# A graph network on one core: GpSimd's gathers wait for the whole group in front from the first column on, and for a count of used columns

## What is computed

```python
x = x + gat(h)        # two graph attention layers (3 heads x 32, then 1 x 32), softmax over the edges of a dst
x = x + rgcn(h)       # two relation passes, 8 relations: mean per (dst, relation), times W[r], summed
x = x + dynamics(h)   # msg = w * h[src] * h[dst] / (5 + 0.9 h[src] + 0.1 h[dst]), summed at src
x = x + relation(h)   # msg = (h[src] @ W_rel[type]) * e, summed at dst, 90 relation types
```

## Time and profile before

| What | us |
|---|---|
| median of 3 runs (lowest, highest) | 6640.55 (6635.97, 6644.13) |
| span of the profiled execution, first to last instruction | 6645.3 |
| GpSimd busy | 4320.0 (65%) |
| VectorE busy | 3659.5 (55%) |
| TensorE busy (matmuls) | 2965.9 (45%) |
| ScalarE busy | 1167.0 (18%) |
| mean of a gather: GAT 1, GAT 2, relation pass 1, pass 2, layer 4 | 1.097, 1.062, 1.058, 1.002, 1.001 |

### The profile page before, as it was taken

How to read it: one execution, slowest core, us unless ns; L and a number is a source line. 1 busy time by engine, 2 the same in 40 slices (tenths; PEclk the granted TensorE clock), 3 DMA queues, 4 the chain that set the end, 5 groups by cost and what they waited for, 6 DMA issues and landing times. The chain is left out here.

```text
span 6645.3 us, 44822 instructions
## 1 busy us (share of the span) xinstructions
PE 2965.9 (45%) x13056; PEld 2260.1 (34%) x13056; DVE 3659.5 (55%) x8917; ACT 1167.0 (18%) x1912; POOL 4320.0 (65%) x3949
## 2 busy tenths in 40 slices
PE   5798699974444344447655443111111002544000
PEld 2477555543333233346644333111111001433000
DVE  8855499976555566654347667433322068876000
ACT  0265454532222233211111100000000000000000
POOL 4666555557762776376657665888888823766776
PEclk9899899985666555556667665555555555776555
DMA  2122222221110322123222212222222234211001
GB/s 41 22 62 70 56 67 67 66 66 12 20 17 14 89 60 65 47 64 100 84 87 60 64 53 72 52 36 36 44 27 27 5 96 154 57 50 37 7 7 44
DMA packets 283354, 350.11 MB, mean 53 GB/s; under 512 B 133518, under 2 KB 204432, under 8 KB 281970
## 3 DMA queue, kind: packets, MB, share of 16 engines
q1 hardware_dynamic: 112158, 295.24, 13.2%
q0 software_dynamic: 169376, 41.40, 7.8%
q10 hardware_dynamic: 1576, 10.60, 0.7%
HBM read 231.06 MB, written 122.29 MB: 53 GB/s over the span
## 5 line engine op out<-in xcount | busy, mean ns | idle before, releaser
L2352 POOL DMA_INDIRECT acc<-l_rows,l_uniq x392 | 624.1, 1592 | 121.0 <-issue 108.6
L2573 POOL DMA_INDIRECT l_ring<-t_last,idx x392 | 392.4, 1001 | 366.5 <-ACTq L2568 207.6
L521 POOL DMA_INDIRECT pay<-in_x,gidx x392 | 460.1, 1174 | 235.4 <-DMA pay<-in_x,gidx 114.3
L2393 PE MATMUL ps_l<-l_msg,l_alike 128*128 128x16 f32 x784 | 176.3, 376 | 962.4 <-DVE l_msg L2456 962.4
L1487 POOL DMA_INDIRECT g_ring<-t_gat,idx x392 | 416.1, 1062 | 278.7 <-issue 110.1
L1817 POOL DMA_INDIRECT r_ring<-t_rel,idx x392 | 414.6, 1058 | 254.6 <-issue 110.3
L809 POOL DMA_INDIRECT t_sort<-pay,c_pos x392 | 384.8, 982 | 296.3 <-DVE c_pos L875 196.3
L901 PE MATMUL ps_c<-plane,c_hit 128*128 128x400 f32 x1568 | 542.6, 499 | 1.2 <-ACT c_hit L827 1.2
L2128 POOL DMA_INDIRECT r_ring<-t_rel,idx x392 | 392.7, 1002 | 224.4 <-issue 110.4
L2338 POOL DMA_INDIRECT l_ring<-t_mix,idx x392 | 426.3, 1087 | 154.6 <-issue 119.1
L2393 PEld LDWEIGHTS ps_l<-l_msg,l_alike 128*128 128x128 f32 x784 | 171.0, 331 | 967.7 <-DVE l_msg L2456 967.7
(11 more groups left out here) (529 smaller groups left out, 8145.0 us busy)
## 6 DMA issues: line engine op xcount, KB each, us to landing
c_rows_d<-row_dst SPq DMA_DIRECT2D x98, 256.0 KB, 3.3
l_keys<-row_at SPq DMA_DIRECT2D x49, 512.0 KB, 4.2
l_typs<-row_typ SPq DMA_DIRECT2D x49, 512.0 KB, 3.7
g_hs<-t_gat SPq DMA_DIRECT2D x30, 660.0 KB, 4.7
acc<-r_zero SPq DMA_DIRECT2D x60, 320.0 KB
t_rel<-r_row SPq DMA_DIRECT2D x30, 640.0 KB, 3.5
r_hs<-t_rel SPq DMA_DIRECT2D x30, 640.0 KB, 4.7
d_gain<-acc SPq DMA_DIRECT2D x30, 640.0 KB, 6.0
```

The lines of the kernel that those rows point to most:

```text
L521: pool.indirect_dma_start(pay[:, s, 8:PAY], None, x, bass.IndirectOffsetOnAxis(gidx[:, s:s + 1], 0)).then_inc(gat_in[s // BATCH], 16)
L2352: pool.indirect_dma_start(acc[r], bass.IndirectOffsetOnAxis(uniq[:, s:s + 1], 0), rows[:, (s // ES) % RR, s % ES, :], None, compute_op=ALU.add
L2573: pool.indirect_dma_start(ring[:, s, :], None, t_last, bass.IndirectOffsetOnAxis(idx2[:, s:s + 1], 0)).then_inc(gat_in[s // BATCH], 16)
```

## The change

`RUN` becomes 0: the wait is for the group directly in front at every eighth column, from the first possible one on. A new helper `credit` adds, at each eighth column past a lead, a wait for a count of used columns: at most `lead` columns are asked for beyond those used. It stands ahead of `paced` in GAT 1 (96 columns, by blocks of 48 mixed), GAT 2 (64, by blocks of 40), relation pass 1 (64, by 8), relation pass 2 (32, by 4) and layer 4 (40, by 8). The ring holds go. The node stage and layer 3 get the new `RUN` alone.

```diff
-RUN = 160
+RUN = 0
...
+def credit(engine, used, s, lead, per):
+
+    if s % BATCH == 0 and s > lead:
+        engine.wait_ge(used, -(-(s - lead) // per))
...
                     for s in range(EARLY, T):
+                        credit(pool, mix_ok, s, 2 * EW, EW)
                         paced(pool, gat_in, s, EARLY)
...
                     for s in range(T):
-                        if s % QN == 0 and s >= NR * QN:
-                            hold(pool, ring_free, s // QN - NR + 1)
+                        credit(pool, ring_free, s, 64, QN)
                         paced(pool, gat_in, s)
...
                         for s in range(T):
-                            if s % QN == 0 and s >= NR * QN:
-                                i = s // QN - NR
-                                hold(pool, expand_ok, first[i] + subs[i])
+                            credit(pool, expand_ok, s, 64, ES)
                             paced(pool, gat_in, s)
...
                     for s in range(T):
-                        if s % QN == 0 and s >= NR * QN:
-                            i = s // QN - NR
-                            hold(pool, lift_ok, first[i] + subs[i])
+                        credit(pool, taken, s, 32, ES)
                         paced(pool, gat_in, s)
...
                     for s in range(T):
+                        credit(pool, mats_used, s, 40, ES)
                         paced(pool, gat_in, s)
```

## The result

The changed kernel takes 6881.51 us (median of 4 runs, 6878.73 to 6890.48), the kernel before in the same comparison 6642.34 (4 runs). The ratio is 1.0366, interval 1.0351 to 1.0381: 239 us more. The forecast was 6909 us, range 6820 to 6945: 28 us high. The profiled execution took 6881.99 us with a span of 6880.0.

The account below looks back on a forecast made before the run. GpSimd's gathers were taken to bound all five streams, so each delay ends its stage later. Landing waits of 188 us plus credits of 81 make 269, added to the median 6640.55: 6909 us, range 6820 to 6945.

Parts of the forecast that it names:

- What bounds each stage: GpSimd's gathers set the end of all five streams; in the node stage VectorE's end covers 4 us, 4 come through.
- GAT 1, layer 3 and layer 4, landing waits: New waits for the group in front cost 17 us in GAT 1, 14 in layer 3, 34 in layer 4.
- GAT 2, landing waits: First groups, behind a 5.6 MB load, cost 12.6 us and the 16 groups after 22.4: together 35.
- stalls rival: Gathers of the five streams meet VectorE less and give back at most 234 us, so 6594 us; chance 0.02.
- Relation passes, landing waits: 19 new waits in each pass at 2.05 and 2.39 us cost 39 and 45 us; 26 each by the lowest price.
- Credits: A second wait costs about 0.45 us at each place in the five streams although long met: 81 us.
- can pass meanwhile: Relation pass 2's credits: 12 of 18 us taken, as the 0.45 us can pass while a load delays a landing.
- That credits never hold GpSimd: In the five streams every used count is reached before its gather, by 24.8 us at the tightest, in relation pass 2.
- Lockstep: Rival: each chunk's store and load meet a landing, relation passes pay 3.5 us a wait, 48 more, 6957 us; chance 0.06.
- absorbed: Rival: the engines behind the gathers have slack, so late gathers cost nothing and it stays at 6640 us; chance 0.02.

Follow-up runs that it names:

- e7: The changed kernel with the landing wait put ahead of the credit wait in the five streams, on a quick chip: 6794.74 us, 1.0232 of the kernel before.
- e6: The changed kernel, unchanged, run again on a quick chip: 6881.38 us, 1.0359 of the kernel before.
- e5: The kernel before, unchanged, run again on a quick chip for its trace: 6640.61 us.
- e12: The changed kernel, credits included, with its landing wait moved to columns with remainder 4, on a slow chip: 7411.22 us, 0.9525 of the kernel before.
- e3: The changed kernel with the landing wait ahead of the credit wait, on a slow chip: 6771.81 us, 0.869 of the kernel before.
- e8: The kernel before with the landing wait for the group in front moved to columns with remainder 4, on a quick chip: 6454.35 us, ratio 0.9721.

## Why the prediction was right, and where its steps were not

Total, sign and the split were right: 154 us for the landing waits against 188, 87 for the credits against 81. It rested on a stage-by-stage reading of who waits last, and that stood: no stage absorbed anything. That the credits came out within 6 us is partly luck, as layer 4 at 18 us too much and relation pass 2 at 20 us too little cancel. Step by step:

- **What bounds each stage.** Right for the five streams. Wrong in the node stage, where I let VectorE's 1543.1 set the end and so took 4 us. It lost 9.0, all of GpSimd's delay. Behind the last gather the raw events show a wait for its landing (to 1538.87) and then a drain of 4.63 us (1539.06 to 1543.69, in the changed kernel 1548.58 to 1553.20) before the block may end. GpSimd set the end in both; VectorE's idle time before its next operation grew from 1.93 to 10.99 us. I had read only the busy instructions.
- **GAT 1, layer 3 and layer 4, landing waits.** 17, 14 and 34 forecast, 19.3, 13.7 (over layer 3's first 80 gathers) and 35.9 measured.
- **GAT 2, landing waits.** The gaps at the eighth columns grew from 8.9 + 54.7 to 48.9 + 49.7 us, exactly the 35 of the sum, with the first groups as worked out. But the gathers' mean fell from 1.063 to 1.030 us, and 392 of those are 12.9 us: the stalls rival, which I had given 0.02 and argued away with two halves of one stream, was true in part: in e7 it gave back 12 us over the five streams, nearly all in GAT 2. Of the 37 us in the changed kernel of the first comparison it is the smaller share; from e7 to e6 the gathers' busy time falls by another 23 us, 19 of them in layer 4, where the credits move the gather past VectorE's operation.
- **Relation passes, landing waits.** Mis-sized: 39 and 45 against 19.2 and 27.2. The price taken was the mean over the paced half (2.05 and 2.39 us), which holds the late landings: in the trace of e5, relation pass 1 has seven gaps over 3 us in its 29 waits. I took it that the new waits would meet as many. In e7 there are four in 48: gaps below column 160 grew by 30.8 us and those above it shrank by 13.2. Late landings belong to the traffic that they meet, and did not multiply with the waits. The lowest price, 26 us each, was nearer.
- **Credits.** The price was right (0.46 us in the medians of layer 4's gaps, 1.65 to 2.11; 0.48 from landing to gather at every place) and so was its reason in outline. By stage it was not even: layer 4, where the delay let the gather miss VectorE's operation, cost 1.4 instead of 19; relation pass 2 cost 32.0 instead of 12. There the mean gap from column 160 on rose from 2.52 to 3.25 us, more than the wait. What I deducted as "can pass meanwhile" does not pass: the 0.74 us begin at the landing, however late it is. The rest are landings that came later still (from the last gather's start to its group's landing 3.55 us in e7, 3.81 in e6, means of the 22 groups that can be read); why they do was not tried. GAT 2 cost 27.9 instead of 16, of which 6.2 are slower gathers (1.030 to 1.046 us).
- **That credits never hold GpSimd.** Right on the quick chips: the gather follows its landing by the same 0.74 us (at most 1.05) at every place with a credit. On a slow chip it is wrong (e12, 56.2 us).
- **Lockstep, absorbed.** Neither happened on the whole; relation pass 2's credits are what there is of the first.

The range was fit for the chips of the first comparison. It says nothing of the slow chips. The changed kernel did not run there; e3's 6772 and 87 us more for the order would be an estimate of 6860, some 12% below the kernel before on such a chip. By that estimate the change gives back on such a chip several times what it costs on a quick one, if the loss is there without the recording.

No version was best everywhere: e8 with 6454 us is the fastest measured on a quick chip, e3 with 6772 on a slow one. On the slow ones e8 was not run; with credits the same wait gave 7411.

## What to carry to other kernels

Pace a stream by a group that has had time to land: the same wait four gathers later cost nothing, where right behind its group it cost 1.3 us or more each time. If two waits precede an instruction, put the one that will be late first and the one already met behind it; here that was 87 us. And before a lead of many gathers is called free, measure it on more than one chip, and look at the other engines' idle time. Where a chip loses much, first compare how many events its trace holds with a trace from a chip that doesn't: the recording may be what costs. Only after that can a limit on what is in flight be called worth more than it costs.

## What the runs showed of the hardware that was not expected

- A gather whose late landing wait is an instruction of its own starts 0.74 us after the landing, one on which that wait rides 0.26 us after it (145 of 148 places of e6, all 143 of e7).
- On two chips TensorE and VectorE fell to one instruction in 1.40 us in stretches while GpSimd gathered without a pause, and TensorE's signals came up to 77 us after the end of its work; the kernel before took some 1150 us more there. With at most 8 gathers in flight nothing of the kind was seen. The traces of these chips lack 29% to 51% of the semaphore updates, so the recording is not excluded as the cause.
- At the end of the node stage GpSimd needs 4.63 us for a drain after its last gather has landed.
